# Fewer zero matmuls in the Householder steps that carry an outer product

## The reference

```python
deg = jnp.sum(A, axis=0) + jnp.sum(A, axis=1) - jnp.diagonal(A)
L_norm = d_inv_sqrt[:, None] * (jnp.diag(deg) - A) * d_inv_sqrt[None, :]
_, U = jnp.linalg.eigh(L_norm)
agg = jnp.einsum('mn,bnd->bmd', U.T, features)
out = jax.nn.relu(agg @ W1 + b1) @ W2 + b2
return jnp.einsum('nm,bmd->bnd', U, out)
```

## Time and profile before

| | us |
|---|---|
| median of 3 runs | 4192.28 |
| lowest, highest run | 4189.59, 4192.59 |
| profiled execution, span | 4189.8 |
| TensorE matmuls busy | 3382.9 (81%) |
| VectorE busy | 3298.6 (79%) |
| ScalarE busy | 1532.1 (37%) |
| zero matmuls (L206), 2875 recorded | 845.9 |

### The profile page before, as it was taken

The page is one execution under the profiler, slowest core; times in us unless marked ns, Lnnn a source line. Parts: engine busy times, 40 slices in busy tenths (PEclk is TensorE's granted clock), DMA queues, the critical chain, the costliest instruction groups (busy, mean ns, idle before and its releaser), DMA issues. The chain is left out here.

```text
span 4189.8 us, 62612 instructions
## 1 busy us (share of the span) xinstructions
PE 3382.9 (81%) x14639; PEld 2049.1 (49%) x14827; DVE 3298.6 (79%) x21659; ACT 1532.1 (37%) x5534; POOL 55.6 (1%) x71
## 2 busy tenths in 40 slices
PE   5999999999999999988886576554207999998859
PEld 3555555555555665577774322243103444454337
DVE  7888898889988788999988899999984323454467
ACT  2444444333333333333332322211212324554545
POOL 0000000000000000000000000000000000020000
PEclk9999999999999899955559887755558999999969
DMA  0000000000000000000000000000002000000001
GB/s 11 1 1 1 1 1 1 1 1 1 1 1 1 1 2 2 1 1 1 1 1 1 1 1 1 1 1 1 0 20 50 0 0 0 1 0 0 0 6 36
DMA packets 14163, 16.47 MB, mean 4 GB/s; under 512 B 571, under 2 KB 10214, under 8 KB 13798
## 3 DMA queue, kind: packets, MB, share of 16 engines
q1 hardware_dynamic: 13798, 12.48, 1.1%
HBM read 8.28 MB, written 4.19 MB: 3 GB/s over the span
## 5 line engine op out<-in xcount | busy, mean ns | idle before, releaser
L206 PE MATMUL ps<-zero_stream 128*128 128x512 bf16 x2875 | 845.9, 397 | 9.0 <-issue 2.8
L206 PEld LDWEIGHTS ps<-zero_stream 128*128 128x128 bf16 x3045 | 333.6, 126 | 227.7 <-issue 101.7
L304 ACT ACTIVATE refl<-ps,tiny 128x1 f32<-128x1 f32 x511 | 133.5, 261 | 451.4 <-PE ps L244 287.9
L318 ACT ACTIVATE vectors<-WihT,refl 128x4 f32<-128x4 f32 (+2 forms) x383 | 115.0, 300 | 391.9 <-DVE refl L439 387.3
L255 PEld LDWEIGHTS ps<-dot_parts,ones 128*128 128x128 f32 x766 | 133.2, 201 | 203.6 <-DVE dot_parts L433 179.9
L233 PE MATMUL ps<-ident,vectors 128*128 128x128 f32 x1148 | 214.9, 298 | 14.3 <-DVE vectors L486 1.3
L380 DVE CUSTOM_DVE_ANT_0 products<-ps,UT 128x511 f32<-128x511 f32 (+60 forms) x426 | 215.0, 533 | 13.1 <-PE ps L233 12.5
L486 DVE SCALAR_TENSOR_TENSOR vectors<-x_scaled,ps,y_scaled 128x4 f32<-128x4 f32 (+3 forms) x510 | 116.2, 228 | 134.5 <-PE ps L255 89.9
L233 PEld LDWEIGHTS ps<-ident,vectors 128*128 128x128 f32 x1148 | 124.0, 141 | 191.6 <-DVE vectors L486 186.0
L380 DVE CUSTOM_DVE_ANT_0 products<-ps,U 128x499 f32<-128x499 f32 (+57 forms) x402 | 199.2, 524 | 5.1 <-PE ps L233 4.6
L686 ACT ACTIVATE sturm_signs<-sturm_products,sign_bias 128x576 bf16<-128x576 f32 x96 | 74.4, 775 | 350.8 <-DVE products_mark L713 350.8
(11 more groups left out here) (611 smaller groups left out, 8440.9 us busy)
## 6 DMA issues: line engine op xcount, KB each, us to landing
out_dram<-x SPq DMA_DIRECT2D x16, 256.0 KB, 2.3
adj<-in_adj_dram SPq DMA_DIRECT2D x1, 1024.0 KB, 5.2
l2w_in<-in_L_gnn_W_dram SPq DMA_DIRECT2D x2, 128.0 KB
Wqkv<-in_L_gnn_Wqkv_dram SPq DMA_DIRECT2D x1, 192.0 KB
L_gnn_W<-in_L_gnn_W_dram SPq DMA_DIRECT2D x2, 64.0 KB
L_gnn_Wg<-in_L_gnn_Wg_dram SPq DMA_DIRECT2D x2, 64.0 KB
x<-in_x_dram SPq DMA_DIRECT2D x4, 0.5 KB
L_gnn_Wo<-in_L_gnn_Wo_dram SPq DMA_DIRECT2D x1, 64.0 KB
```

The lines of the kernel that those rows point to most:

```text
L206: nc.tensor.matmul(MA[t][:],still[:,0:P],still[:],start=False,stop=True,skip_group_check=True)
L304: nc.scalar.activation(s[:,u,Y:Y+1],NG[:,0:1] if wide else NG[:,1:2],ACT.Sqrt,bias=tiny[:,0:1]).then_inc(root,1)
```

## The change

One table of `streams` is edited. The second number of zero matmuls in a kind-1 step is 2, 2 and 1 by block, and was 6, 5 and 4. All else is as it was.

```diff
     b=m//P; kind=2 if ends_panel(m) else 3 if m>PANEL and m%PANEL==1 else 1 if update_tile(m) else 0
     if b==NT-1: return (0,0,0)
-    return (1 if b<2 else 0,((6,6,9,6),(5,5,4,4),(4,4,3,5))[b][kind],2)
+    return (1 if b<2 else 0,((6,2,9,6),(5,2,4,4),(4,1,3,5))[b][kind],2)
```

## The result

The changed kernel takes 4307.74 us (median of 4 runs, 4287.81 to 4315.35), the one before 4190.93 us (4 runs, 4149.99 to 4192.59). The ratio is 1.0295, 95% interval 1.0245 to 1.0344: 2.9% slower. The profiled execution has a span of 4302.9 us and a time of 4305.01.

A forecast was written before the change was run, and what follows sets the result against it. Bound: the Householder step chain (VectorE dot parts, TensorE sum, VectorE next column), its dot delayed by zero matmuls, and TensorE's clock. Path -21.7 us and clock +112 us gave +90 on 4189.8, 4280, stated as 4282; range 4180 to 4370.

The forecast's parts named there:

- The gain at full clock: Kind-1 steps: the dot is on time again, winning 0.30, 0.17 and 0.08 us per step by block, 21.7 us.
- The clock falls in nearly every panel: Householder stage: some 43 of 47 panel stretches below full clock instead of 21; block clocks about 0.87, 0.88, 0.74.
- To rise only in the first plain step or later: Carrying steps of a panel: once fallen, the clock recovers only after them, in the first plain step or later.
- The time at half clock: Householder stage: 175, 143 and 288 us at half clock by block after the change, against 68, 45 and 89 before.
- The price per us at half clock: Householder stage after the change: 0.32, 0.32 and 0.31 us lost per us at half clock, by block; cost 191 us.
- The bound with the falls of the kernel before: Householder stage with only the present falls: 198 us at half clock cost 65 us, a change of -14 us.
- TensorE waited only 0.70 us: First carrying step of a panel: the clock fell after a 0.70 us wait, so waiting alone isn't the cause.
- C: Rival: the clock doesn't come back between panels, half the stage runs at half clock; +177 us, 4369; chance 0.15.
- D: Rival: dot no earlier because its parts come later too; no direct cost, +112 us, 4304; no chance apart.
- Rival A: Householder stage: the clock holds as now, -21.7 of path and -14 of shorter cold steps; 4156 us; chance 0.10.
- B: Rival: only block 2 pays in clock, falls in blocks 0 and 1 unchanged; +24 us, 4216; chance 0.17.

The follow-up runs named there:

- The smaller cut: The kernel before with 4, 4, 3 zero matmuls by block instead of 6, 5, 4 in kind-1 steps; 4180.32 us, ratio 1.003.
- the narrow matmuls: The changed kernel with each removed zero matmul replaced by a one-column float32 matmul of zeros ahead of the dot wait; 4517.25 us, ratio 1.0853.
- the change on the combined kernel: The combined kernel with 2, 2, 1 zero matmuls instead of 4, 4, 3 in kind-1 steps; 4220.08 us, ratio to the kernel before 1.0107.
- the combined kernel: The kernel before with three zero matmuls behind every dot, 3, 2, 1 more in panels' first steps, and 4, 4, 3 in kind-1 steps; 4096.82 us, ratio 0.9807.

## Why the prediction was right

The forecast was 4282 us, the measured 4307.74, inside the range and slower as said. The mechanism is the one forecast: a small gain on the path and a larger loss in clock. The size is partly luck, since two terms of the loss were off in opposite ways. Step by step:

- The gain at full clock, 21.7 us: confirmed. 0.30 us per step in block 0 by rows; over all kind-1 steps at full clock 5.35 to 5.04 us in block 0, 4.47 to 4.31 in block 1, 3.69 to 3.67 in block 2, with only 5, 2 and 4 such steps left. The smaller cut has more of them, 26, 27 and 14, and takes 5.06, 4.31 and 3.62 us; that makes 0.29 x 45 + 0.16 x 33 + 0.07 x 32 = 21 us.
- The clock falls in nearly every panel: confirmed. A fall begins in 44 of the 47 panels, and in the other three the clock is still low, where I said 43. The blocks' clocks are 0.84, 0.85 and 0.71, a little lower than the 0.87, 0.88 and 0.74 forecast.
- "To rise only in the first plain step or later": wrong. In the first panel the clock rose inside a kind-1 step and fell again in the next: the middle row of that panel above has 0.78 between 0.65 and 0.50. Of the 50 rises 13 are in a kind-1 step, 8 of them in block 0, and so there are 21 falls in block 0's 15 panels, where I had counted 14.
- The time at half clock was the term that I knew least, and it was sized too small: 222, 177 and 317 us against 175, 143 and 288. In block 1 I had put it in the kind-1 steps alone, and eleven of its plain steps ran at half clock from end to end.
- The price per us at half clock: 0.32, 0.32, 0.31 assumed. Without falls the stage would be 1739.9 - 79 - 21.7 = 1639 us by the prediction's own terms; 1854.7 - 1639 = 216 us over 716 us is 0.30. With its own prices the prediction would have had 226 us for these 716 us, and a span of 4189.8 - 79 - 21.7 + 226 = 4315 us, 12 too many: the price was a little too high (11 us), the time at half clock too short by 110 us (35 us at these prices), and the second error was the larger. (The bound with the falls of the kernel before has 198 x 0.32 = 65 us; that is 63, and nothing hangs on it.)
- That "TensorE waited only 0.70 us" in the first step of a panel holds for the step of the earlier trace rows; in most of those of block 0 it waits near 0.98 us. The conclusion, that waiting isn't what brings the clock down, doesn't hang on it: the narrow matmuls and the change on the combined kernel show it.
- C, with half the stage at half clock and +177 us, was approached in length (716 of 870 us), less so in time (+117 us). The clock failed to come back between panels in three stretches of block 2 only.
- D has the time closest to the measured one, 4304 us, and is false all the same: the dot is earlier, 0.06 us behind its parts where it was 0.64. That its number fits is chance.
- Rival A, the clock holds as it does now, had 0.10; the blocks' clocks show it false, and the narrow matmuls show that idle gaps don't decide. B had the right order of blocks (block 2 pays most, 56 us) but the other two pay too.

## What to carry to other kernels

Filler matmuls that compute nothing can be worth more than the time that they take on the path: before cutting some, count how long the engine is at half clock now, and look at which matmuls it would be left with around the cut. Cut only as far as the waiting instruction behind them gets on time, and put filler where the engine waits anyway; here that and the smaller cut together gained 1.9%, the large cut lost 2.9%. A step's path gain read at full clock is an upper bound that holds only if the clock does.

## What was not expected of the hardware

With narrow float32 matmuls in the place of the wide ones TensorE was busy for 8.86 of 9.07 us, and its clock fell right behind; over the whole stage of that run the mean was 0.75.

The same kernel before took from 4146.70 to 4192.59 us over all its runs, 46 us in 34 runs; the combined kernel, with few falls, kept within 8.5 us in its four. The longer runs had less clock: in one session the longest, 4188.11 us, was granted 0.841 over the span and the shortest, 4158.47, 0.855. So the spread goes with the falls of the clock, as far as these means show, and single runs of this kernel can't tell 1%. The three runs from which the prediction starts lie at the upper end of it; against the 4169.31 to 4178.46 us of the later sessions the change costs 129 to 138 us, and not 117, if the chips are alike.
